# Dense experts for the last group of tokens, and both probability copies on ScalarE in part of phase one

## What is computed

```python
shared = (silu(x @ sw1) * (x @ sw2)) @ sw3
probs  = softmax(x @ rw + rb)
w, idx = top_k(probs, 2);  w = w / sum(w)
gates  = sum(w[..., None] * one_hot(idx, 8))            # zero for six of the eight
h      = silu(x @ ew1[e]) * (x @ ew2[e])                # for every expert e
routed = sum_e gates[..., e] * (h[e] @ ew3[e])
return shared + routed
```

## Time and profile before

| | |
|---|---|
| median of 3 runs | 2207.82 us (2199.66 to 2215.62) |
| profiled execution | 2207.8 us, of which the span is 2206.0 us |
| mean granted clock of PE | 0.943 of full |
| PE busy | 1864.3 us (85%) |
| PE weight loads | 1526.4 us (69%) |
| DVE busy | 1507.5 us (68%) |
| ACT busy | 1273.2 us (58%) |
| POOL busy | 632.0 us (29%) |
| units of phase one (line 1203) | first at 45.4 us, last at 875.6 us |
| last attention unit of phase three (line 2376) | 2082.2 us |
| from there to the end of the span | 124 us |

### The profile page before, as it was taken

The page is one execution under the profiler, slowest core; times in us unless marked ns, Lnnn a source line. Parts: engine busy times, 40 slices in busy tenths (PEclk is TensorE's granted clock), DMA queues, the critical chain, the costliest instruction groups (busy, mean ns, idle before and its releaser), DMA issues.

```text
span 2206.0 us, 50221 instructions
## 1 busy us (share of the span) xinstructions
PE 1864.3 (85%) x17706; PEld 1526.4 (69%) x17706; DVE 1507.5 (68%) x3921; ACT 1273.2 (58%) x4415; POOL 632.0 (29%) x626
## 2 busy tenths in 40 slices
PE   3987988888889989657788889999999988888874
PEld 2776886777778767436666677777777776777664
DVE  5998776777877898566676665767757574745352
ACT  1765655556566667436677756666667654545421
POOL 0003020231411220014343433254443424242321
PEclk9998998999999999868899989999999999999997
DMA  7013334453454200310000011222222222223253
GB/s 235 16 30 100 109 117 134 130 171 106 139 149 134 76 22 7 113 57 19 29 6 15 6 42 38 84 80 83 79 73 66 80 83 87 86 82 95 86 163 113
DMA packets 125127, 184.22 MB, mean 84 GB/s; under 512 B 10320, under 2 KB 82064, under 8 KB 124624
## 3 DMA queue, kind: packets, MB, share of 16 engines
q1 hardware_dynamic: 116688, 164.23, 24.5%
q0 software_dynamic: 8192, 16.79, 2.5%
HBM read 145.52 MB, written 35.45 MB: 82 GB/s over the span
## 4 chain that ended last, share of the span: by engine, by line
PE 34%; DVE 8%; issue 6%; ACT 6%; POOL 2%; DMA 1%; SPq 0%; DVEq 0%; ACTq 0%; POOLq 0%
PE ps L1633 5%; PE ps L1885 4%; PE ps L1866 3%; ACT pb L2031 3%; PE ps L1859 3%; PE ps L1671 3%; PE ps L1655 3%; PE ps L1662 2%; PE ps L1840 2%; PE ps L1644 2%; DVE nm L2376 2%; PE ps L1681 1%; PE ps L1689 1%; PE ps L1832 1%; DVE hT L2169 1%
## 5 line engine op out<-in xcount | busy, mean ns | idle before, releaser
L2031 ACT ACTIVATE pb<-ps,nm 128x128 f32<-128x128 f32 x1024 | 364.0, 378 | 196.9 <-DVE nm L2376 196.9
L2072 POOL TENSOR_TENSOR pb<-pb,rcs 128x512 f32<-128x512 f32 x256 | 268.6, 1050 | 669.1 <-DVE rcs L2384 668.3
L978 ACT ACTIVATE pb<-pb,nm 128x128 f32<-128x128 f32 x1024 | 313.0, 392 | 83.3 <-DVE nm L1203 83.2
L2401 DVE COPY pt<-ps 128x512 f32<-128x512 f32 x128 | 88.4, 690 | 203.6 <-PE ps L1885 203.1
L2031 ACT ACTIVATION_READ_ACCUMULATOR pb<-ps,nm 128x1 f32 x1024 | 222.1, 217 | 0.0
L2376 DVE TENSOR_REDUCE nm<-ps 128x8 f32<-128x1024 f32 x128 | 155.9, 1218 | 65.0 <-PE ps L1866 41.8
L1885 PE MATMUL ps<-w,pb 128*128 128x128 f32 x1024 | 166.9, 288 | 22.8 <-ACT pt L2039 10.9
L1633 PE MATMUL ps<-hT,big 128*128 128x128 f32 x960 | 137.1, 288 | 27.3 <-DVE hT L2174 14.5
L1203 DVE TENSOR_REDUCE nm<-pb 128x8 f32<-128x1024 f32 x128 | 156.2, 1220 | 4.4
L1633 PEld LDWEIGHTS ps<-hT,big 128*128 128x128 f32 x960 | 123.2, 199 | 48.7 <-issue 24.8
L865 PE MATMUL ps<-w,pb 128*128 128x128 f32 x1024 | 147.5, 286 | 8.2 <-ACT pb L978 7.7
(11 more groups left out here) (369 smaller groups left out, 4386.8 us busy)
## 6 DMA issues: line engine op xcount, KB each, us to landing
big<-in_we SPq DMA_DIRECT2D x92, 514.0 KB
big<-in_we SPq DMA_DIRECT2D x120, 384.0 KB
big<-sorted_in SPq DMA_DIRECT2D x8, 960.0 KB, 5.7
sorted_out<-big SPq DMA_DIRECT2D x28, 256.0 KB
sorted_in<-big SPq DMA_DIRECT2D x4, 1472.0 KB, 12.2
sorted_out<-h_all SPq DMA_DIRECT2D x16, 256.0 KB
hidden<-h_all SPq DMA_DIRECT2D x7, 512.0 KB, 3.0
h_all<-hidden SPq DMA_DIRECT2D x7, 512.0 KB, 3.8
```

The lines of the kernel that those rows point to most:

```text
L978: m = a.activation(pb[:, n % 2, k * S:(k + 1) * S], pb[:, n % 2, k * S:(k + 1) * S], ACT.Exp, bias=nm[:, n % 2, k:k + 1])
L2031: m = a.activation(pb[:, n % 2, e * S:(e + 1) * S], ps[:, score_bank(n) + half, k * S:(k + 1) * S], ACT.Exp, bias=nm[:, n % 2, e:e + 1], a ...
L2072: g_.tensor_tensor(p4, p4, r4.unsqueeze(2).to_broadcast([P, 4, S]), ALU.mult).then_inc(n2["p_normed"], 1)
L2401: v.tensor_copy(pt[:, p % 2, 4 * S:8 * S], ps[:, BANK_T, :]).then_inc(n2["p_lo"], 1)
```

## The change

**In phase one**, in every unit for which no tile is scheduled, ACT copies the second half of the transposed probabilities right after the first, and DVE doesn't. In units with tiles it stays as it was.

**In phase three** groups 0 to 6 (ND = 7) are worked as before. Group 7 isn't ranked, scattered, tiled or gathered. All nine experts, the shared one first, run over all its 512 rows, which PE has turned already (`yTm`): `dense("hidden", i)` is half of an expert's hidden part (128 of 256) for 512 rows, `dense("output", e)` its output for all four batches, which DVE adds to x, times the gate of that expert (zero for rows that don't use it). This runs at unit 165, after group 6's window, in the order `DENSE_STEPS`. The weights of experts 1 to 4 come in one load into the space of layer 3's query, key and value weights, which is issued at unit 151; those of 5 to 8 go into the four slots of the tiles' weights. Group 6's combination is put behind the output of expert 6. The last unit becomes 172 instead of 182.

```diff
 # phase one, ScalarE
                         a.activation(pt[:, p % 2, 0:4 * S], ps[:, 2, :], ACT.Copy).then_inc(s["p_hi"], 1)
+                        if not any(tiles_at(place, n) for place in range(3)):
+                            a.wait_ge(s["transposed"], 2 * p + 2)
+                            a.activation(pt[:, p % 2, 4 * S:8 * S], ps[:, 3, :], ACT.Copy).then_inc(s["p_lo"], 1)
 # phase one, VectorE
-                    if 0 <= n - 1 < NUN:
+                    if 0 <= n - 1 < NUN and any(tiles_at(place, n) for place in range(3)):
...
 # phase three, the plan
+        NDW = E3 - NW3
+        ND = NG - 1
-        for g in range(NG):
+        for g in range(ND):
...
+        DENSE_AT = tiles_from[-1] + len(window[-1]) + 1
+        COMBINE_AFTER = 6
+        DENSE_STEPS = [("hidden", h) for h in range(4)]
+        for e in range(E3 + 1):
+            DENSE_STEPS += [("output", e)] + [("hidden", h) for h in range(2 * e + 4, min(2 * e + 6, 2 * E3 + 2))]
...
+        dense_w = [shared3] + [big[:, e * WT3:(e + 1) * WT3].rearrange("p (w c m) -> p w c m", w=3, c=C3) if e < NDW
+                               else w3[:, (NT * ND + e - NDW) % NW3] for e in range(E3)]
+        dense_u = [slot512(13), slot512(14)]
+        dense_h = [[slot512(15 + 2 * k + c) for c in range(C3)] for k in range(2)]
+        dense_banks = [(0, 1), (BANK_T, BANK_PV), (BANK_X, BANK_Z)]
 # SyncE
+                    if g == ND:
+                        sp.dma_start(ws3[:, k % NW3, :], we3_d[NDW + t, :, :]).then_inc(weights_loaded[k % NW3], 16)
+                        return
...
+                    if hs == L3_AT[NG - 1][IC3 - 1]:
+                        sp.wait_ge(n2["v_psum"], IC3 * NG)
+                        sp.dma_start(big[:, 0:NDW * WT3].rearrange("p (e n) -> p e n", e=NDW),
+                                     we3_d[0:NDW, :, :].rearrange("e p n -> p e n")).then_inc(loaded[0], 16)
 # TensorE
-                    if g is not None and place == 0:
+                    if g is not None and g < ND and place == 0:
                         bank_b((moe["index"], g + 1))
                         rank_pe(pe, sort3[g], sel_z[:, G:PB + 1, :], BANK_B, g + 1)
...
+                def dense(kind, i):
+                    if kind == "hidden":
+                        e, c = divmod(i, 2)
+                        if i == 0:
+                            pe.wait_ge(experts.yT_ready, NG)
+                            pe.wait_ge(moe["hid_dve"], NTILE * ND)
+                            pe.wait_ge(n2["o_read"], len(units))
+                        if i == 2:
+                            pe.wait_ge(moe["turned_back"], NQ * ND)
+                        if i >= 3:
+                            pe.wait_ge(moe["hid_dve"], NTILE * ND + i - 2)
...
+                        for half, bank in enumerate(dense_banks[i % 3]):
+                            m = pe.matmul(ps[:, bank, :], dense_w[e][:, half, c, :], yTm[:, :], start=True, stop=True)
+                        m.then_inc(moe["hid_psum"], 1)
+                    if kind == "output":
+                        pe.wait_ge(moe["hid_dve"], NTILE * ND + 2 * i + 2)
...
+                        if i >= 2:
+                            pe.wait_ge(moe["b2_added"], ND + i - 1)
+                        for b in range(G):
+                            for c in range(C3):
+                                m = pe.matmul(ps[:, (BANK_A, BANK_B)[i % 2], b * D:(b + 1) * D],
+                                              dense_h[i % 2][c][:, b * S:(b + 1) * S], dense_w[i][:, 2, c, :],
+                                              start=(c == 0), stop=(c == C3 - 1))
+                        m.then_inc(moe["expert"], 1)
 # ScalarE
+                        for i in range(2 * E3 + 2):
+                            a.wait_ge(moe["hid_psum"], NTILE * ND + i + 1)
+                            if i >= 2:
+                                a.wait_ge(moe["hid_dve"], NTILE * ND + i - 1)
+                            a.activation(dense_u[i % 2], ps[:, dense_banks[i % 3][0], :], ACT.Tanh, scale=0.5)\
+                                .then_inc(moe["silu"], 1)
 # VectorE
+                    if g is not None and g < ND and place == 1:
                         rank_dve(v, link, sort3[g], sel_z[:, G:PB, :], BANK_B, g + 1)
...
+                def dense(kind, i):
+                    x = x_group(NG - 1)
+                    if kind == "hidden":
...
+                        v.scalar_tensor_tensor(dense_u[i % 2], dense_u[i % 2], 1.0, ps[:, gate_bank, :], ALU.add, ALU.mult)\
+                            .then_inc(moe["gated"], 1)
...
+                        v.scalar_tensor_tensor(dense_h[e % 2][c], ps[:, up_bank, :], 0.5, dense_u[i % 2], ALU.mult, ALU.mult)\
+                            .then_inc(moe["hid_dve"], 1)
+                    if kind == "output":
...
+                            for b in range(G):
+                                m = v.scalar_tensor_tensor(x[:, b, :], ps[:, bank, b * D:(b + 1) * D],
+                                                           gates[:, b, i - 1:i], x[:, b, :], ALU.mult, ALU.add)
...
+                    if hs == DENSE_AT:
+                        for kind, i in DENSE_STEPS:
+                            dense(kind, i)
+                            if (kind, i) == ("output", COMBINE_AFTER):
+                                combine(ND - 1)
```

More of the change, by code:

```diff
@@ L1436, in build @@
         hidden_order = [item[0::2] for _, _, item in order if item[1] == "hidden"]
-        assert hidden_order == [(g, i) for g in range(NG) for i in range(NTILE)]
+        assert hidden_order == [(g, i) for g in range(ND) for i in range(NTILE)]
         assert [item[0::2] for _, _, item in order if item[1] == "output"] == hidden_order
@@ L1532, in load_weights @@
                     g, t = divmod(k, NT)
-                    if t == 0 or k < NW3:
+                    if g < ND and (t == 0 or k < NW3):
                         sp.wait_ge(moe["tiles"], g + 1)
@@ L1571, in _ @@
                         for g, kind, i in tile_items(place, hs):
-                            if kind == "output" and i >= NSH and NT * g + i - NSH + NW3 < NT * NG:
+                            if kind == "output" and i >= NSH and NT * g + i - NSH + NW3 < NT * ND + NW3:
                                 load_weights(NT * g + i - NSH + NW3)
@@ L1586, in _ @@
                             .then_inc(out_stored, 16)
-                sp.wait_ge(moe["stored"], 16 * NQ * NG)
+                sp.wait_ge(moe["b2_added"], ND + E3 + 1)
+                sp.dma_start(out_d.rearrange("b s d -> s b d")[:, (NG - 1) * G:NG * G, :], x_group(NG - 1))\
+                    .then_inc(out_stored, 16)
+                sp.wait_ge(moe["stored"], 16 * NQ * ND)
             @block.tensor
@@ L1869, in scores @@
                     m.then_inc(n2["scores"], 1)
+                def dense(kind, i):
[9 more added lines that the diff above has]
+                            pe.wait_ge(moe["hid_dve"], NTILE * ND + i - 2)
+                        if c == 0 and e == 1:
+                            pe.wait_ge(loaded[0], 16 * (NG // 2 + 1))
+                        if c == 0 and e > NDW:
+                            k = NT * ND + e - 1 - NDW
+                            pe.wait_ge(weights_loaded[k % NW3], 16 * (k // NW3 + 1))
+                        for half, bank in enumerate(dense_banks[i % 3]):
[3 more added lines that the diff above has]
+                        pe.wait_ge(moe["hid_dve"], NTILE * ND + 2 * i + 2)
+                        if i == 0:
+                            pe.wait_ge(moe["logit_row"], NG)
+                            pe.wait_ge(n2["chunk_added"], IC3 // 2 * NG)
+                        if i >= 2:
[6 more added lines that the diff above has]
+                        m.then_inc(moe["expert"], 1)
                 for hs in range(FIRST, LAST + 1):
@@ L2102, in _ @@
                         g = moe_at(hs, 5 + k)
-                        if g is not None:
+                        if g is not None and g < ND:
                             if k == 0:
@@ L2124, in _ @@
                                     .then_inc(moe["gathered"], 16)
-                g_.wait_ge(moe["gathered"], 16 * 2 * G * NG)
-                g_.wait_ge(moe["scattered"], 16 * 2 * G * NG)
+                g_.wait_ge(moe["gathered"], 16 * 2 * G * ND)
+                g_.wait_ge(moe["scattered"], 16 * 2 * G * ND)
             @block.vector
@@ L2365, in work @@
                     g = find([at + 5 for at in GATHER_AT], hs)
-                    if g is not None and place == 2:
+                    if g is not None and g < ND - 1 and place == 2:
                         combine(g)
+                def dense(kind, i):
+                    x = x_group(NG - 1)
+                    if kind == "hidden":
+                        e, c = divmod(i, 2)
+                        gate_bank, up_bank = dense_banks[i % 3]
+                        v.wait_ge(moe["silu"], NTILE * ND + i + 1)
```

(18 more changed lines are left out.)

## The result

The changed kernel takes **2164.51 us** (median of 4 runs, 2163.07 to 2170.7); the kernel before, on the same chip, 2204.52 us (4 runs, 2199.66 to 2215.62). The ratio is **0.9831, 95% interval 0.9801 to 0.986**: 40 us less. 39 were forecast. On another chip the same two kernels gave 2173.5 and 2201.94 us, ratio 0.9871 (0.9844 to 0.9899): 28 us less, and that interval (some 22 to 34 us) leaves the 39 out. The gain is real on both chips; its size is known only to some 6 us either way.

What follows compares the result with a forecast made beforehand. DVE was taken as the tight engine in phase one's copy stretches, PE hardly less, and a chain of latencies at the end. 2207.8 - 24 (dense last group) - 15 (copies) = 2169 us, range 2151 to 2190.

Steps and rivals of the forecast that it cites:

- What a removed copy is worth: Phase one, units without tiles: each copy taken off DVE saves 0.73 us, gap included; 39.6 us in all.
- The cap by ACT: Phase one, units without tiles: ACT needs 3.97 us in every unit, so a 3.36 us unit rises by 0.61.
- costs nothing by itself: Phase one: ACT's new wait for the transposes' second half is covered by its copies of 0.36 and 0.58 us.
- The factor 0.39: Phase one: three units gain 0.85 us instead of 2.19; this share of 39.6 us gives 15 us, range 4 to 26.
- Units 30 to 33: Before the first tile: POOL sets the pace, so DVE's gain after 196 us is lost waiting; first tile near 213 us.
- The start of the last group: End of phase three: without group 7's ranking operations on DVE, the chain of tiles runs 1.3 us earlier.
- The big load: Last group's weights: SP's 1,536 KB load from unit 151 is free; without SP's gap, up to 8 us.
- The stream: Last group: nine dense experts bound by PE, 49.3 us, 5.5 each; the end comes 24 us earlier.
- DVE alone bounds phase one: Rival, phase one: all 39.6 us of the copies come back, total 2144 us; chance 0.08.
- ACT takes DVE's place: Rival, phase one: ACT limits the short units, copies gain 4 us or none, total 2180 to 2184; chance 0.17.
- The stream doesn't stutter: Denies the rival that PE waits about 1 us per dense expert for DVE: +9, 2178 us; chance 0.10.
- The slow clock: Rival, last group: dense stream held at 1.2 GHz, end 25 us later than before, total 2218 us; chance 0.03.

Runs made afterwards that it cites:

- the kernels without fillers: Changed kernel without TensorE's three filler products per unit of phase one without tiles: 2170.43 us, ratio 0.9846; also with ScalarE's new copy cut to 16 columns: 2170.05 us.
- copy last: Changed kernel with ScalarE's new copy moved behind its other copies of the unit, just ahead of the exponentials: 2163.34 us, ratio 0.9841 to the kernel before.
- all three kernels that ran there: The kernel before, 2307.26 us; the changed kernel with ScalarE's new copy cut to 16 columns, 2264.29 us; the one with both remedies, 2265.51 us.
- both remedies: Changed kernel with ScalarE's new copy behind its other copies and group 6 combined after expert 4's output: 2265.51 us against 2307.26 before, ratio 0.9823.

## Why the prediction was right

**What a removed copy is worth: term mis-sized.** The prediction took 0.68 + 0.05 = 0.73 us. In units that stay DVE's the unit falls by 0.60: unit 16 from 7.55 to 6.95, unit 112 from 4.38 to 3.78, unit 107 from 7.69 to 7.09. The timeline of the kernel before shows where the rest is. DVE's rows overlap:

```profile
771.97 0.68 DVE L1210 COPY pt<-ps 128x512 f32<-128x512 f32 x1
772.56 0.20 DVE L1181 RECIPROCAL rc<-ps 128x8 f32<-128x8 f32 x1
```

The copy has 0.68 us, but the next instruction starts 0.59 after it. 54 copies are then worth 32 us, not 39.6.

**The cap by ACT: right in a few units, for the rest it stood in for something else.** The lengths came out much as foreseen. The three units of the earlier trace rows gained 0.67 us together, forecast 0.85; 23 rose from 3.91 to 4.50, where +0.61 was forecast for 3.36, and 106 from 3.36 to 3.91. But the reason given, that ACT needs 3.97 us in every unit, holds only in part. Units 104, 108, 112 and 120 are below it, at 3.78, and DVE's. In 106 and 114 ACT's load does hold the unit (shown at full clock in the kernels without fillers). Units 10, 15, 23, 123 and 125 keep their length when the new copy is cut to 0.18 us. In the changed kernel DVE is idle for 0.9 to 1.6 us in each of them, waiting for PE, so one copy less on DVE shortens them no further. That the way from the exponentials over transposes, value products and scores back to DVE sets their length is argued from these waits, not tested. The sentence that ACT's new wait "costs nothing by itself" was wrong in three units: ACT's other copies queue up behind the new one in 102, 110 and 118, 0.48 us each.

**The factor 0.39: about right, by luck.** By single units that neither the clock nor the start disturbs, the change saves 4.0 us in 102 to 126 (113.21 to 109.18; without 109 and 117) and 5.9 in 0 to 28 (100.44 to 94.51; without 1, 2, 18 to 20 and 26 to 28). That is 9.9 us for 44 units (9.6 against the two other profiles with the old copies), where 0.60 in each would be 26: a factor of 0.38. It was read from three units and from ACT's load; that the other units lose as much, few of them by ACT's load, is luck. The marks give 189.3 to 181.4 us (means of the three kernels with the old copies and of four with the new) and 125.5 to 119.8 (the latter without copy last), 13.6 in all, and the run with the copies alone 12. The difference to 9.9 lies in the units left out, most of it by the clock as far as can be read. In the kernel before unit 117 takes 6.77 us and falls into this window (granted clock 0.62):

```profile
828.00:835.00 7.00, 7.00 (x53) 5.37 (x52) 3.80 (x6) 4.06 (x13) 0.61 (x1) 0.62 0.01 2
```

In the changed kernel its twin, unit 109, takes 6.61 at 0.69, and 117 takes 4.03 at 1.00:

```profile
779.70:786.40 6.70, 6.70 (x54) 4.91 (x54) 2.93 (x6) 4.50 (x13) 0.00 (x0) 0.69 0.00 0
821.20:825.30 4.10, 4.10 (x48) 2.95 (x47) 2.91 (x5) 3.98 (x12) 0.00 (x0) 1.00 0.02 8
```

Which unit is hit differs from kernel to kernel; the two together cost 12.75 us before, 11.46 with the dense part alone, 10.64 after, and 9.4 to 13.5 in the others (8.1 on chip C, where other units are disturbed). The prediction's sum had no such term.

**Units 30 to 33: right.** From unit 29 to 35 it takes 41.93 us before and 41.97 after. What DVE wins is waited for at the first tile, which starts at 217.1 us (221.6 before; the prediction had 213: it expected some 8 us from the first stretch, and POOL starts 5.2 earlier, at 190.79). The changed kernel's waits of PE, 195 to 225 us, where the earlier trace rows has 5.97 us:

```profile
PE ps L741 <- DMA big<-sorted_in: 7.1, 1, 7.1
```

**The start of the last group: right.** From the last maxima to group 6's last output it takes 46.3 us before and 44.9 after: 1.4, forecast 1.3.

**The big load: right.** SP issues it at 2057.07, 16 us before its next loads, and among the waits of the stream none is for a DMA, but POOL's for its gather:

```profile
2057.07 0.38 SPq L1585 DMA_DIRECT2D big<-in_we  x1
2073.01 6.63 SPq L1558 DMA_DIRECT2D big<-in_we  x3
```

**The stream: one term mis-sized, the structure right.** An expert takes 5.22 us, not 5.5. The eight small products were forecast at 1.88 and come to 1.78 (5.22 less 3.44). The product of 512 columns, at 3.44 / 4 = 0.86, was forecast at 0.90, and lies in its bounds of 0.82 to 0.94. The wait ahead of the last output is 1.02 us (6.4 against 5.5 in the forecast, 0.9). From group 6's last output to the last addition's end it takes 50.1 us, forecast some 51, and 74.8 before. With the earlier start the end gains 26 us (marks: 124.7 to 98.5 on average), forecast 24.

**The rivals.** DVE alone bounds phase one (2144): refuted by unit 106 and by the 12 us. That ACT takes DVE's place is closer: it happens in 106, 114 and three others, not everywhere, and the copies alone gained 12 us and not 4 or none. The stream doesn't stutter. The slow clock didn't come; PE had no pause, and in all ten profiles with the dense stream the granted clock is 1.00 throughout it, where the kernel before has a mean of 0.73 from 2130 to 2206 us. The Trainium skill's rule that waits between bursts bring it down ("TensorE: Matmul & The Clock Gate", HAM oscillation) goes with both: 1.00 in the stream without waits here, 0.50 after the pause in the earlier trace rows.

So the 39 us came out as 40, from 15 and 24 that were 12 and 28 by the medians, each to some 6 us. The end rests on a mechanism that the runs bear out term by term. The copies' 15 us rest on a copy priced too high and on a cap by ACT that holds in few units; two terms were wrong in opposite directions, that copy and a product shorter than assumed.

## What to carry to other kernels

Price a removed instruction by the distance from its start to the next one's on its engine, not by its duration and a gap, and only in units where that engine doesn't wait: where it waits for the others, the instruction is worth little or nothing. When work moves to an engine with spare time, count that engine unit by unit, and put the new instruction behind those that others wait for. For a last step with a long chain of latencies, dense work that keeps one engine full can cost less than sparse work behind waits: here 9 experts on all 512 rows took 50 us where sorted tiles, stores and gathers took 75.

## What was unexpected on the chip

Neighbouring DVE rows overlap by 0.08 to 0.10 us (the copy of 0.68 us, followed after 0.59).

Filler products can be worth their PE time: without them the granted clock fell from 1.00 to 0.86 and from 0.83 to 0.66 in two stretches, and the kernel wasn't faster, although units 102 to 127 took 117.1 us for 119.8.

Two profiles of one program differed by 10 us in phase three (1102.0 and 1112.3), most of it in one stretch of low clock. With that spread a gain of 2 us can only be read from single units.

On chip C all three kernels that ran there took some 4.6% longer, the one before 2307.26 us, with the same ratio between them. In phase one there are stretches there in which DVE is idle for up to 13 us and PE runs products one by one, most of them among the tiles, some outside (units 31 and 105). A window of the kernel with both remedies on that chip:

```profile
466.00:493.00 27.00, 13.27 (x82) 8.80 (x83) 7.30 (x15) 6.21 (x18) 16.93 (x18) 0.63 0.23 64
```

and its DVE in it:

```profile
491.36 1.23 DVE L582 TENSOR_TENSOR pb<-ps,mask1i 128x1024 f32<-128x1024 f32 x1 [13.06 <-remote]
```

PE's rows lie one by one in it, most after a pause of 0.2 to 1.7 us put down to "issue", while POOL's scatters and gathers run evenly. The pauses stand at the same units, with nearly the same lengths, in both profiles from that chip (11.3 and 11.2 us at unit 31, 13.1 at 62, 10.2 at 80). Units 35 to 102 took 595.1 and 596.1 us in place of 513.3 to 520.8. That the engines are fed their instructions late there is a guess; the cause was not tested and stays open.
